# Two edits in an LSTM decoder's step: another order of two waits on ScalarE, and four output-gate matmuls placed behind the attention's gate products

## The reference, cut to what matters

```
def attend(h):
    q = h @ Wq.T
    scores = jnp.einsum('bc,bsc->bs', q, context)
    alpha = jax.nn.softmax(scores, axis=-1)
    ctx = jnp.einsum('bs,bsc->bc', alpha, context)
    return jnp.tanh(jnp.concatenate([ctx, h], axis=-1) @ Wout.T + b_out)

def step(carry, x_t):
    h, c, attn = carry
    inp = jnp.concatenate([x_t, attn], axis=-1)
    gates = inp @ W_ih.T + b_ih + h @ W_hh.T + b_hh
    i, f, g, o = jnp.split(gates, 4, axis=-1)
    c = jax.nn.sigmoid(f) * c + jax.nn.sigmoid(i) * jnp.tanh(g)
    h = jax.nn.sigmoid(o) * jnp.tanh(c)
    attn = attend(h)
    return ((h, c, attn), attn)
```

## Time and profile before

| what | value |
|---|---|
| median of 3 runs | 5745.92 us (5745.6 to 5747.82) |
| the profiled execution's own time | 5744.19 us |
| its span in the trace | 5742.4 us |
| busy, TensorE matmul / VectorE / ScalarE / GpSimd | 91% / 60% / 35% / 6% |
| LSTM loop | 512 steps, from about 190 to 3937 us of the span |

### The profile page before, as it was taken

How to read it: one execution, slowest core, us unless ns; L and a number is a source line. 1 busy time by engine, 2 the same in 40 slices (tenths; PEclk the granted TensorE clock), 3 DMA queues, 4 the chain that set the end, 5 groups by cost and what they waited for, 6 DMA issues and landing times. The chain is left out here.

```text
span 5742.4 us, 383675 instructions
## 1 busy us (share of the span) xinstructions
PE 5219.3 (91%) x171240; PEld 3816.0 (66%) x171240; DVE 3449.3 (60%) x15922; ACT 1998.5 (35%) x7977; POOL 350.1 (6%) x795
## 2 busy tenths in 40 slices
PE   9899999999999999999999999998688879797989
PEld 4677777777777777777777777776444434343433
DVE  5455555555555555555555555554798999999931
ACT  2244444444444444444444444442222222223221
POOL 0000000000000000000000000000121211212100
PEclk9999999999999999999999999999799889898999
DMA  2000000000000000000000000002111101010111
GB/s 99 35 2 2 2 2 2 2 2 2 2 2 2 2 2 2 2 2 2 2 2 2 2 2 2 2 2 81 50 52 41 42 18 54 25 54 25 56 37 54
DMA packets 45677, 111.60 MB, mean 19 GB/s; under 512 B 8192, under 2 KB 10240, under 8 KB 45072
## 3 DMA queue, kind: packets, MB, share of 16 engines
q1 hardware_dynamic: 44144, 109.39, 6.2%
q10 hardware_dynamic: 1440, 1.06, 0.1%
HBM read 99.90 MB, written 10.52 MB: 19 GB/s over the span
## 5 line engine op out<-in xcount | busy, mean ns | idle before, releaser
L857 PE MATMUL lstm_part_ps<-lstm_keys,lstm_hid 128*4 128x128 f32 x32768 | 1024.9, 273 | 207.0 <-DVE lstm_hid L1029 207.0
L857 PEld LDWEIGHTS lstm_part_ps<-lstm_keys,lstm_hid 128*4 128x4 f32 x32768 | 771.1, 86 | 430.0 <-DVE lstm_hid L1029 416.2
L873 PE MATMUL lstm_ctx_ps<-lstm_values,lstm_alpha 128*4 128x128 f32 (+1 forms) x49152 | 1051.7, 237 | 0.5 <-issue 0.5
L873 PEld LDWEIGHTS lstm_ctx_ps<-lstm_values,lstm_alpha 128*4 128x4 f32 x49152 | 903.0, 86 | 89.4 <-issue 0.7
L1053 DVE TENSOR_REDUCE lstm_neg_max<-lstm_part_ps 128x1 f32<-128x128 f32 x1024 | 299.1, 292 | 679.0 <-PE lstm_part_ps L857 679.0
L1011 DVE STREAM_TRANSPOSE lstm_gates<-lstm_half_ps 128x96 f32<-128x96 f32 x1026 | 290.6, 283 | 567.7 <-PE lstm_half_ps L816 543.8
L989 ACT ACTIVATE lstm_expo<-lstm_part_ps,lstm_neg_max 128x128 f32<-128x128 f32 x1024 | 376.3, 367 | 648.5 <-DVE lstm_neg_max L1053 648.5
L816 PE MATMUL lstm_half_ps<-lstm_w_hid,lstm_hid 128*13 128x96 f32 x16384 | 563.8, 245 | 0.0
L816 PE MATMUL lstm_half_ps<-lstm_w_attn,lstm_attn 128*13 128x96 f32 x16448 | 434.8, 246 | 1.3 <-issue 1.3
L2090 ACT ACTIVATE mix_gated<-mix_gate_ps 115x512 f32<-115x512 f32 (+2 forms) x200 | 112.6, 563 | 777.7 <-PE mix_gate_ps L1818 772.8
L978 ACT ACTIVATE lstm_cell<-lstm_gates 128x12 f32<-128x12 f32 x1024 | 224.8, 220 | 411.1 <-DVE lstm_gates L1011 411.1
(11 more groups left out here) (326 smaller groups left out, 8236.0 us busy)
## 6 DMA issues: line engine op xcount, KB each, us to landing
mix_ring<-in_sm_chunks SPq DMA_DIRECT2D x120, 358.0 KB, 2.9
mix_ring<-in_mix_chunks SPq DMA_DIRECT2D x80, 384.0 KB, 3.0
lstm_xg<-xg_rows SPq DMA_DIRECT2D x514, 16.0 KB
xg_rows<-rec_lam SPq DMA_DIRECT2D x16, 512.0 KB, 2.6
xT<-in_xT SPq DMA_DIRECT2D x4, 512.0 KB, 8.4
ctxT<-in_ctxT SPq DMA_DIRECT2D x1, 2048.0 KB, 14.1
out_xT<-xT SPq DMA_DIRECT2D x4, 512.0 KB, 3.8
lstm_w_x<-in_lstm_w_x SPq DMA_DIRECT2D x1, 1024.0 KB, 17.4
```

Source lines behind the costliest of these rows:

```text
L857: mm = pe.matmul(part_rows(score_ps[part], b), hid[:, k, lo:lo + SPACE], keys[:, k, b * SRC + c * P:b * SRC + (c + 1) * P], start=(n == 0 ...
L873: mm = pe.matmul(part_rows(ctx_ps[n], b), alpha[:, b, c, SPACE - 1 - c:2 * SPACE - 1 - c], values[:, b * SC + c, ctx_cols[n]], start=(c == ...
```

## The change

On ScalarE the wait for `attn_kept` moves behind the wait for `attn_summed[0]`, so that the first tanh of the attention still waits for both, in the other order. On TensorE the output gate's product of h's second chunk (one `gate_sums`, 8 records of 64 columns) leaves its place ahead of the wait for `attn_ready[0]` and goes to the head of `o_gate_attn`, behind the four `half_attn` products. No instruction is added or taken away, and no sum has other terms.

```
-                def o_gate_x_hid(u):
+                def o_gate_hid(c):
+
+                    gate_sums(o_gate_ps, o_cols, hid[:, c, PAD:PAD + ROWS], w_hid[:, c, :])
 
+                def o_gate_x_hid(u):
+
                     gate_sums(o_gate_ps, o_cols, place, xg[:, u, :], start=True).then_inc(xg_used, 1)
-                    for c in range(KC):
-                        gate_sums(o_gate_ps, o_cols, hid[:, c, PAD:PAD + ROWS], w_hid[:, c, :])
+                    o_gate_hid(0)
 
                 def o_gate_attn():
 
+                    o_gate_hid(1)
                     for c in range(KC):
                         mm = gate_sums(o_gate_ps, o_cols, attn[:, c, 0:ROWS], w_attn[:, c, :], stop=c == KC - 1)
                     mm.then_inc(o_ready, 1)
...
-                        act.wait_ge(attn_kept, t + 1)
                         for o in range(KC):
                             act.wait_ge(attn_summed[o], t + 1)
+                            if o == 0:
+                                act.wait_ge(attn_kept, t + 1)
                             act.activation(by_batch(attn[:, o, :]), attn_ps[o], ACT.Tanh).then_inc(attn_ready[o], 1)
```

## The result

The changed kernel takes 5774.33 us, the kernel before 5745.6 us (medians of 5 runs each). The ratio is 1.0050 with a 95% interval of 1.0040 to 1.0061: slower by 28.7 us. 5771 was predicted, in a range of 5758 to 5785. The profiled execution took 5772.62 us with a span of 5770.8, both 28.4 above those of before; the granted clock in the loop is 1.00 as before.

What follows compares the result with a forecast made beforehand. The prediction took each of 512 steps to be a chain through TensorE, ScalarE and VectorE. A 0.10 us later output gate, less slack, left 0.05 a step: 5745.9 + 25.6 = 5771.5, kept as 5771, range 5758 to 5785.

Steps and rivals of the forecast that it cites:

- The loop and nothing else: Whole kernel: a step's gain or loss counts 512 times; nothing outside the loop changes; 25.6 us more.
- The order of the waits: ScalarE, attention: the first tanh gains 0.06 us, the second nothing; the wait for `attn_kept` runs early for nothing.
- The rival in which it runs through: Attention's tanh: both halves start 0.06 us sooner; 5746, or 5715 if absorption held too; chance 0.05, 0.03 with both.
- The product in front hid two waits: TensorE: first attention product 0.07 us sooner, holes of about 0.05 before both products, both halves gain only 0.01.
- 0.10 later at the output gate's tanh: ScalarE: the moved product's 0.11 us less the halves' 0.01 delays the output gate's tanh by 0.10.
- Slack of 0.04 in front of the transpose: VectorE: the output gate's transpose could have started 0.04 us sooner, so it comes only 0.06 later.
- Slack of 0.01 at h's wait: VectorE, half 0's new h: the separate wait for `o_turned` leaves 0.01 us of slack, so h is 0.05 late.
- the 0.12 that I had named as a sign: VectorE: h starting much sooner than 0.12 us behind the output gate's transpose would show the prediction wrong.
- The late gate absorbed: At h: a separate wait costs under 0.06 us, so the step gains 0.01; 5741 us; chance 0.10.
- The unbuffered rival: VectorE: the slack before the transpose is missing, so the whole 0.10 us reaches h; 5797 us; chance 0.10.
- From h to the step: VectorE to TensorE: half 1's cell, tanh and h and the scores come as late as half 0's h, 0.05 us.
- The sum: Whole loop: 512 x 0.05 = 25.6 us more on 5745.9, giving 5771.5, of which 5771 was kept.

Runs made afterwards that it cites:

- the early x part: Kernel before with the new order of waits, output gate's x part made behind the next step's x products, in its own PSUM bank: 5742.88 us, ratio 0.9992.
- the half of the columns: Changed kernel with only 32 of the 64 output gate columns of h's second product, in all four quarters, moved behind: 5746.08 us, ratio 1.0003.

## Why the prediction was right, step by step

One row of the kernel before is needed beside the earlier trace rows. It lies between the two rows shown there:

```profile
2010.37 0.16 DVE L1077 RECIPROCAL lstm_inverse<-lstm_total_sum 128x1 f32<-128x1 f32 x1
```

- **The loop and nothing else.** Right: 7.373 against 7.318 us a step, times 512, is 28 us of 28.7.
- **The order of the waits gives the first tanh 0.06 us, and this is worth nothing.** Right, in the table above and in the run of that edit alone (ratio 0.9999). The rival in which it runs through fell with the early x part, where TensorE was free: the ratio was still 0.9992 (0.9983 to 1.0001), and the rival's 5715 would be 0.995.
- **The product in front hid two waits.** Right: the first attention product starts 0.07 sooner, the second, held by the second tanh, 0.01. What is left of it for both halves is 0.003 at half 0's transpose (median), a little less than my 0.01.
- **0.10 later at the output gate's tanh.** It was 0.11.
- **Slack of 0.04 in front of the transpose.** 0.045 by the medians, and shown as a threshold by three sizes of the moved part. But the sign that I had named for it, an idle time of VectorE in front of the transpose, isn't there: the row of the cell update in front lasts until 2011.86 and overlaps the transpose's start at 2011.84. What shows the wait is the distance from one start to the other, 0.14 instead of 0.08, and the 0.03 from the tanh's end.
- **Slack of 0.01 at h's wait, which is a separate instruction.** Right in kind, and in size partly by luck. Without h's wait the loss was gone in the changed kernel and nothing changed in the kernel before. But I had the 0.01 as 0.13 less 0.12, two distances that were each set by the other wait of their instruction: the 0.13 by the cell's tanh, and the 0.12 of the earlier trace rows by the reciprocal, which I didn't look at. It ends at 2010.53, 0.05 in front of `sel_scaled`, so neither distance was the price of a separate wait. The price is 0.104, a little under the 0.12 that I had named as a sign, the distance before was 0.117, and the slack 0.013 (medians). My range had left 0.02 for it.
- **The late gate absorbed** (5741). This rival needed a price under 0.06. The rule of the Trainium skill named beside it ("VectorE: DVE Perf Modes", "The DRAIN you can't avoid") was measured on copies with a semaphore after each. Here a carried wait takes 0.033 and the separate one 0.104, so the runs don't agree with it for a wait that stands alone.
- **The unbuffered rival** (5797) fell with the result itself and with the half of the columns, at ratio 1.0003.
- **From h to the step.** I had half 1's h and the scores as late as half 0's h because half 1's cell is queued behind it on VectorE. Right: half 1's h is 0.060 late, and with its cell moved in front the step no longer hung on it.
- **The sum** was 0.05 us a step; 28.7 / 512 = 0.056 was measured. The 0.006 too little is in the terms of the tanh (0.106, not 0.10) and the transpose, which I took at its old length and which takes 245 ns instead of 236. By the medians the sum is 0.106 - 0.045 + 0.009 - 0.013 = 0.057: the two delays were 0.015 larger than I had them, and the two slacks took 0.008 of that back.

## What to carry to other kernels

Work that is moved behind a critical product is free only up to the slack of the sum it belongs to; find the slack link by link (here 0.045 us at a transpose and 0.013 at the next wait) before moving 0.11. To read the price of a wait from a distance, check first that the instruction's other wait had come earlier. Filling TensorE's idle time in front of a wait cost nothing here, and taking the filler away won nothing, since a later wait, that for the second tanh, held the chain. Where two things come out at the same moment, as the cell's tanh and the output gate did here, look at what is queued behind the instruction that waits for both: taking half 1's cell out from behind it was worth 13 us, where one of the two edits gave nothing and the other cost 29.

## What the runs showed of the hardware that was not expected

- The four quarter matmuls of a product, each on its own 32 partitions of the output, run side by side: with two of the four moved, the tanh behind was 0.08 us late, and with half of the columns of all four, 0.05.
- The same transpose takes 245 ns in the changed kernel, where it starts 0.03 us behind the end of the tanh that it waits for, and 236 in the kernel before, where the tanh had ended 0.08 us earlier and the start came 0.08 behind that of the cell update in front.
- Of h's two waits, the carried one takes 0.033 us from the end of the instruction waited for to h's start, and the separate one 0.104 (medians, VectorE). On ScalarE the first tanh of the attention starts 0.154 behind the start of `select(1)` where `attn_summed[0]` is the separate wait (kernel before), and 0.093 where it is the carried one (changed kernel and the run of that edit alone).
